# A transformer layer on one core: router chain grouped over several pairs, residual add moved into PSUM, both norms of a pair in one step

## The reference, cut to what matters

```
x = layernorm(x + self_attention(x, causal))           # ln1
x = layernorm(x + cross_attention(x, ctx of 77 rows))  # ln2
p = softmax(x @ router_w + router_b)                   # [2048, 8]
topw, topi = top_k(p, 2);  topw = softmax(topw)
out = sum over the two chosen experts of topw * (gelu(x @ w1[e] + b1[e]) @ w2[e] + b2[e])
x = layernorm(x + out)                                 # ln3
```

## Time and profile before

| | us |
|---|---|
| median of 3 runs | 496.29 (495.0 to 496.47) |
| profiled execution, its own time | 500.52 |
| its span, first to last instruction | 498.5 |
| mean granted TensorE clock | 0.896 |
| iterations with SA, CA and router all at work (starts of SA's last ku): | 124.5, 164.2, 200.7, 236.7, 276.4 |
| POOL's first sending of pairs 0 to 7 | 132.6, 172.2, 208.7, 244.7, 284.3, 318.8, 346.6, 371.2 |

### The profile page before, as it was taken

One profiled execution on the slowest core, in us unless ns is written; L12 is line 12 of the kernel. 1 busy time (PEld: TensorE's weight loads), 2 busy tenths in 40 slices (PEclk: granted clock), 3 DMA queues, 4 the chain that ended last, 5 costly groups with the idle time before them and its releaser, 6 DMA issues.

```text
span 498.5 us, 8885 instructions
## 1 busy us (share of the span) xinstructions
PE 371.4 (75%) x2121; PEld 247.8 (50%) x2121; DVE 315.8 (63%) x1061; ACT 282.5 (57%) x648; POOL 171.4 (34%) x217
## 2 busy tenths in 40 slices
PE   2349678989989989989888998856612999999400
PEld 1313444565455555565464554343212999999300
DVE  9732554778767777878768777546362555555282
ACT  2017268679677769679658769626220555555122
POOL 9403111131431342341422341511311354454343
PEclk9967999999997999999989999975955999999855
DMA  6330202521341332341332331040681122221153
GB/s 196 106 74 0 63 23 49 132 54 33 89 123 31 75 122 44 81 125 35 87 105 48 76 122 39 18 129 19 211 234 48 48 68 66 59 61 51 42 135 84
DMA packets 47818, 39.92 MB, mean 80 GB/s; under 512 B 4762, under 2 KB 44559, under 8 KB 47768
## 3 DMA queue, kind: packets, MB, share of 16 engines
q1 hardware_dynamic: 45496, 35.11, 27.0%
q0 software_dynamic: 2272, 4.24, 2.6%
HBM read 13.66 MB, written 14.79 MB: 57 GB/s over the span
## 4 chain that ended last, share of the span: by engine, by line
PE 31%; DVE 22%; issue 10%; DMA 8%; ACT 8%; SPq 7%; DVEq 7%; POOL 3%; another core or an unknown queue 0%; POOLq 0%; ACTq 0%
PE bank L535 7%; SPq L366 6%; PE bank L479 4%; DMA sa_km<-sa_ku 4%; PE bank L522 4%; DVEq L980 4%; PE bank L480 3%; ACT sa_qm L674 3%; PE bank L503 3%; DVE ca_us L983 2%; PE bank L502 2%; PE bank L546 2%; DVE yb L993 2%; DVE ca_nm L810 2%; ACT ca_qm L674 2%
## 5 line engine op out<-in xcount | busy, mean ns | idle before, releaser
L733 ACT ACTIVATE sa_us<-bank,expert_b 128x128 f32<-128x128 f32 x156 | 44.9, 367 | 47.8 <-PE bank L617 36.1
L1051 POOL TENSOR_SCALAR_AFFINE_SELECT sa_pt<-sa_pt 128x512 f32<-128x512 f32 x64 | 38.9, 635 | 75.8 <-ACT sa_pt L682 75.7
L1083 POOL DMA_INDIRECT results<-sa_us,xs x39 | 41.1, 1054 | 51.8 <-DVE sa_us L995 49.5
L810 DVE TENSOR_REDUCE sa_nm<-bank 128x4 f32<-128x512 f32 x64 | 41.5, 684 | 16.9 <-PE bank L503 16.3
L617 PE MATMUL bank<-xsT,ca_us 128*128 128x128 f32 x312 | 45.7, 291 | 2.6 <-DVE ca_us L983 1.6
L1074 POOL DMA_INDIRECT dispatched<-r_sent,r_row x32 | 31.8, 994 | 44.2 <-DVE r_sent L936 36.9
L674 ACT CAST sa_qm<-bank 8x512 fp32r<-8x512 f32 x64 | 36.9, 576 | 13.7 <-PE bank L510 12.1
L617 PEld LDWEIGHTS bank<-xsT,ca_us 128*128 128x128 f32 x312 | 39.4, 198 | 7.2 <-issue 4.0
L628 PE MATMUL bank<-ca_pt,sa_us 128*128 x312 | 41.5, 276 | 0.2 <-issue 0.2
L674 ACT CAST ca_qm<-bank 8x512 fp32r<-8x512 f32 x64 | 36.8, 575 | 8.2 <-PE bank L510 6.9
L682 ACT ACTIVATE sa_pt<-bank 128x512 f32<-128x512 f32 x64 | 34.8, 597 | 10.1 <-PE bank L522 9.9
(11 more groups left out here) (210 smaller groups left out, 855.9 us busy)
## 6 DMA issues: line engine op xcount, KB each, us to landing
dispatched<-filler SPq DMA_DIRECT2D x17, 520.0 KB, 4.5
sa_km<-sa_ku SPq DMA_DIRECT2D x32, 96.0 KB
sa_qm<-sa_qu SPq DMA_DIRECT2D x32, 96.0 KB
ca_qm<-ca_qu SPq DMA_DIRECT2D x32, 96.0 KB
xs<-dispatched SPq DMA_DIRECT2D x39, 65.0 KB
sa_pt<-in_e_w SPq DMA_DIRECT2D x8, 256.0 KB, 4.8
ca_pt<-in_e_w SPq DMA_DIRECT2D x8, 256.0 KB, 5.5
sa_pt<-results SPq DMA_DIRECT2D x8, 256.0 KB, 4.5
```

What stands on the lines that cost most here:

```text
L733: act.activation(hid[b][:, c, :], bank[2 * b + c // 2][:, P * (c % 2):P * (c % 2) + P], ACT.Gelu, bias=b1[:, bass.ds(expert * FC + c, 1)]) ...
L810: dve.tensor_reduce(k.nm[:, u, g, :], bank[home[k, "scores", u][g % 2]][:, :].rearrange("q (j n) -> q j n", j=J)[:, :, 0:k.keys], AX.X, AL ...
L1051: pool.affine_select(out=blockg, in_=blockg, compare_op=ALU.is_ge, fill=0.0, base=0, pattern=[[0, J], [1, P]], channel_multiplier=-1).then ...
L1083: pool.indirect_dma_start(out=results, out_offset=bass.IndirectOffsetOnAxis(ap=xs[v][:, P:P + 1].bitcast(I32), axis=0), in_=ys[v], in_offs ...
```

## The change

Router: the pairs are put in groups (0, 1), (2, 3, 4), (5, 6) and (7). `route` is still done for each pair, and DVE adds the bias to its logits; everything else of the chain, PE's `place` and POOL's sending included, is done once for a group, when its last pair comes to that step, on tiles of 4, 6, 4 and 2 x 8 values. The chain has 27 instructions beside the one for each pair. The running count goes: PE makes it from products of ones with each earlier group's totals (float32) and with the earlier tiles of the group (bf16). `fill` moves from iteration p + 1 to iteration p + 2 and waits for the sending of the group before its own.

Norm: `residual` is multiplied by the identity into PSUM and wo's product is added on top; for CA the bias bo is added in the same way. Statistics are read from PSUM. Both tiles of a pair are one step: SA's where tile 1 was, CA's at the start of iteration p + 2, where tile 1 was. `x1` goes straight into `residual`, and POOL keeps only one `rs` for both tiles.

```diff
+def routed_together(pairs):
+    groups, left = [], list(range(pairs))
+    for size in (2, 3, 2):
+        if len(left) > size:
+            groups.append(tuple(left[:size]))
+            left = left[size:]
+    return groups + [(p,) for p in left]
...
-        ROUTER_OPS = 32
-        SELECTED = 19
+        SHIFTED, SELECTED, RANKED, ROUTER_OPS = 2, 18, 22, 27
...
-            (CA, "norm", 1, -2), (SA, "weights", 0, 0), (SA, "scores", 3, 0), (SA, "weights", 1, 0),
+            (CA, "norm", 0, -2), (SA, "weights", 0, 0), (SA, "scores", 3, 0), (SA, "weights", 1, 0),
...
-            (SA, "norm", 0, 0), (SA, "values", 0, 1), (CA, "mix", 0, -1), (SA, "turn_heads", 1, 0),
-            (CA, "weights", 1, -1), (SA, "norm", 1, 0), (CA, "weights", 2, -1), (RT, "number", 0, -2),
+            (SA, "values", 0, 1), (CA, "mix", 0, -1), (SA, "turn_heads", 1, 0),
+            (CA, "weights", 1, -1), (SA, "norm", 0, 0), (CA, "weights", 2, -1), (RT, "number", 0, -2),
...
-            (CA, "turn", 0, 0), (RT, "fill", 0, -1), (CA, "mix", 3, -1), (SA, "shift", 0, 1), (CA, "norm", 0, -1),
+            (CA, "turn", 0, 0), (RT, "fill", 0, -2), (CA, "mix", 3, -1), (SA, "shift", 0, 1), 
...
             def fill(k, p, u):
-                if after_pair(p):
-                    sp.wait_ge(r.s_disp, p * 64)
+                first = group_of[p][1][0]
+                if first:
+                    sp.wait_ge(r.s_disp, first * 64)
...
             def norm(k, p, u):                                  # PE
-                pe.wait_ge(k.s_ot, p * 2 + u + 1)
                 take(home[k, "norm", u][0])
-                pe.matmul(bank[home[k, "norm", u][0]][:, 0:D], k.oT[:, u, :], k.wo[:, :], start=True, stop=True).then_inc(k.s_w_ps, 1)
-                give(home[k, "norm", u][0], k.s_y, p * 2 + u + 1)
+                both = bank[home[k, "norm", u][0]][:, 0:2 * D].rearrange("q (v d) -> q v d", v=2)
+                pe.matmul(both, ident, residual[:, 2 * p:2 * p + 2, :], start=True, stop=False)
+                if not k.causal:
+                    pe.matmul(both, ident, k.bo.rearrange("q (o d) -> q o d", o=1).to_broadcast([P, 2, D]), start=False, stop=False)
+                for v in range(2):
+                    pe.wait_ge(k.s_ot, p * 2 + v + 1)
+                    ins = pe.matmul(both[:, v], k.oT[:, v, :], k.wo[:, :], start=False, stop=(v == 1))
+                ins.then_inc(k.s_w_ps, 1)
+                give(home[k, "norm", u][0], k.s_xn, p * 2 + 2)
...
             def place(k, p, u):                                 # PE, once for a group of `tiles` tiles
-                pe.matmul(dst, triangle_bf[:, :], r.sel[:, :, :].rearrange("q v e -> q (v e)"), start=True, stop=False)
-                ins = pe.matmul(dst, ones_bf[:, :], r.acc[:, :, :].rearrange("q v e -> q (v e)"), start=False, stop=True)
+                for c in range(TOPK):
+                    ins = pe.matmul(dst, triangle_bf[:, :], r.chosen[:, c, 0:tiles, :], start=(c == 0), stop=False)
+                for m in range(n):
+                    pe.matmul(dst, ones[:, :], r.total[:, m:m + 1, :].to_broadcast([P, tiles, EXPERTS]), start=False, stop=False)
+                for v in range(tiles - 1):
+                    for c in range(TOPK):
+                        last = v == tiles - 2 and c == TOPK - 1
+                        ins = pe.matmul(dst[:, v + 1:tiles, :], ones_bf[:, :], r.chosen[:, c, v:v + 1, :].to_broadcast([P, tiles - 1 - v, EXPERTS]), start=False, stop=last)
...
             def norm(k, p, u):                                  # DVE
+                dve.wait_ge(k.s_w_ps, p + 1)
+                for v in range(2):
+                    dve.bn_stats(k.bs[:, v, 0:6], y[:, v, :]).then_inc(k.s_bs, 1)
+                if after_pair(p):
+                    dve.wait_ge(k.s_rs, p)
+                for v in range(2):
+                    dve.wait_ge(k.s_bs, p * 2 + v + 1)
+                    dve.bn_aggr(k.ba[:, v, :], k.bs[:, v, :]).then_inc(k.s_ba, 1)
+                for v in range(2):
+                    dve.wait_ge(k.s_ba, p * 2 + v + 1)
+                    dve.scalar_tensor_tensor(out=k.xn[:, v, :], in0=y[:, v, :], scalar=k.ba[:, v, 0:1], in1=k.g, op0=ALU.subtract, op1=ALU.mult).then_inc(k.s_xn, 1)
+                dve.wait_ge(k.s_rs, p + 1)
+                for v in range(2):
+                    dve.wait_ge(k.s_xn, p * 2 + v + 1)
+                    dve.scalar_tensor_tensor(out=residual[:, 2 * p + v, :], in0=k.xn[:, v, :], scalar=k.rs[:, v:v + 1], in1=k.b, op0=ALU.mult, op1=ALU.add).then_inc(k.s_x1, 1)
...
             def norm(k, p, u):                                  # POOL
+                pool.wait_ge(k.s_ba, p * 2 + 2)
+                if after_pair(p):
+                    pool.wait_ge(k.s_x1, p * 2)
+                pool.tensor_tensor(k.rs[:, :], k.ba[:, :, 1], half[:, :].to_broadcast([P, 2]), ALU.pow).then_inc(k.s_rs, 1)
             def number(k, p, u):                                # POOL
+                n, group = group_of[p]
+                if p != group[-1]:
+                    return
                 pool.wait_ge(s_filled, p * 32 + 32)
-                pool.wait_ge(r.s_rt, p * ROUTER_OPS + ROUTER_OPS)
+                pool.wait_ge(r.s_rt, (n + 1) * ROUTER_OPS)
                 pool.wait_ge(r.s_xe1, p + 1)
-                pool.wait_ge(CA.s_xr, p * 2 + 2)
-                for v in range(2):
+                for v in range(2 * len(group)):
                     for c in range(TOPK):
                         pool.indirect_dma_start(out=dispatched, ...
```

More of the change, by code:

```diff
@@ L117, in build @@
         r.xT = sb("r_xT", [D, 2 * P])
[L118 to L127, removed]
+        r.lg, r.ls, r.exl, r.p, r.eq, r.key, r.pm, r.eq2, r.key2, r.base = (
+            sb(f"r_by_expert{n}", [P, TILES, EXPERTS]) for n in range(10))
+        r.nmx, r.sm, r.rsm, r.p1, r.km, r.p2, r.km2, r.d, r.ed, r.den = (
+            sb(f"r_by_token{n}", [P, TILES]) for n in range(10))
+        r.chosen = sb("r_chosen", [P, TOPK, TILES, EXPERTS], BF16)
+        r.at = sb("r_at", [P, TOPK, TILES, EXPERTS])
+        r.pos = sb("r_pos", [P, TOPK, TILES])
+        r.total = sb("r_total", [P, len(ROUTED), EXPERTS])
+        ones = sb("ones", [P, P])
+        r.sent = sb("r_sent", [P, TILES, TOPK, ROW])
+        r.row = sb("r_row", [P, TILES, TOPK], I32)
         r.s_xt_ps = sem("r_xt_ps")
@@ L857, in norm @@
[L857 to L865, removed]
+                y = bank[home[k, "norm", u][0]][:, 0:2 * D].rearrange("q (v d) -> q v d", v=2)
@@ L872, in routed, with wide, each @@
                 ins.then_inc(r.s_rt, 1)
[L873 to L879, removed]
+                dve.wait_ge(r.s_rt, group_of[p][0] * ROUTER_OPS + done[0])
+            def wide(t, tiles):
+                return t[:, 0:tiles].rearrange("q (v o) -> q v o", o=1).to_broadcast([P, tiles, EXPERTS])
+            def each(t, tiles):
+                return t.rearrange("q (o e) -> q o e", o=1).to_broadcast([P, tiles, EXPERTS])
             def gate(k, p, u):
+                n, group = group_of[p]
+                t, at = 2 * len(group), 2 * (p - group[0])
                 if not after_pair(p):
@@ new lines, in second @@
+            def second(k, p, u):
+                n, group = group_of[p]
+                if p != group[-1]:
+                    return
+                t = 2 * len(group)
+                routed(p, dve.scalar_tensor_tensor(out=r.pm[:, 0:t, :], in0=r.chosen[:, 0, 0:t, :], scalar=-2.0, in1=r.p[:, 0:t, :], op0=ALU.mult, op1=ALU.add))
+                largest(p, t, r.pm, r.p2, r.eq2, r.key2, r.km2, 1)
+                routed(p, dve.tensor_tensor(r.d[:, 0:t], r.p2[:, 0:t], r.p1[:, 0:t], ALU.subtract))
+                routed(p, dve.tensor_reduce(r.total[:, n, :], r.chosen[:, :, 0:t, :].rearrange("q c v e -> q e c v"), AX.XY, ALU.add))
@@ new lines, in place @@
+                if p != group[-1]:
+                    return
+                t = 2 * len(group)
+                if group[0]:
+                    dve.wait_ge(r.s_disp, group[0] * 64)
+                dve.wait_ge(r.s_exp, n * 2 + 2)
+                routed(p, dve.tensor_scalar(r.den[:, 0:t], r.ed[:, 0:t], 1.0, None, ALU.add))
+                gates = [r.sent[:, 0:t, c, ROW - 1] for c in range(TOPK)]
+                routed(p, dve.reciprocal(gates[0], r.den[:, 0:t]))
+                routed(p, dve.tensor_tensor(gates[1], r.ed[:, 0:t], gates[0], ALU.mult))
@@ new lines, in place @@
+                routed(p, dve.tensor_copy(r.sent[:, 0:t, :, P].bitcast(I32), rows_sb[:, 2 * group[0]:2 * group[0] + t, :]))
+                assert done[0] == RANKED, done[0]
+            def number(k, p, u):
+                n, group = group_of[p]
+                if p != group[-1]:
+                    return
+                t = 2 * len(group)
+                dve.wait_ge(r.s_rank_ps, n + 1)
+                routed(p, dve.tensor_tensor(r.base[:, 0:t, :], bank[home[k, "place", u][0]][:, 0:t * EXPERTS].rearrange("q (v e) -> q v e", v=t), each(region, t), ALU.add))
```

(4 more changed lines are left out.)

155 lines of the change are left out of this document (67 added, 88 removed).

## The result

The changed kernel takes 522.4 us (median of 4 runs, 520.96 to 526.08) where the kernel before took 496.4 beside it (495.0 to 498.17): ratio 1.0512, interval 1.0472 to 1.0552. That is slower by 25.4 us. The prediction was 513.0 with a range of 499 to 521: the sign was right, the size was not, and the time lies 1.4 us outside the range. The profiled execution of after took 520.96 (span 519.2); the one of before took 500.5, 4 us over its median, so the spans of the two traces are only 20.7 us apart. Sizes are therefore taken from the timed ratios (a ratio less 1, times 496.4), mechanisms from the traces. Each ratio is to runs of the kernel before timed beside it and leaves out runs in which the chip was in a slower state, so that it need not match the medians to 3 us.

A forecast was written before the change was run, and what follows sets the result against it. The prediction took in-order PE to pace the iterations. Its terms, 12.9 + 4.1 + 2.8 + 0.7 - 2.0 - 2.2 + 0.4 = +16.7 us, on 496.3 gave 513, range 499 to 521.

The forecast's parts named there:

- stalls and clock: Group-ending iterations 3 and 6: late fills and long sendings delay rs, PE waits 12.9 us; lowered clock afterwards costs 4.1.
- remaining terms: PE's products +2.8, place +0.7, DVE's relief -2.0, between iterations 7 and 8 -2.2, the end +0.4 us.
- The merged norm: Pair's norm on DVE: 2.6 us where tile 1 alone took 1.9; 0.3 left over, inside the products' 0.46.
- PE's products: Added float32 products: SA's hidden, CA's 0.85 us less 0.4 for ca_y, net 0.46 in six iterations, +2.8 us.
- The gain that was set against them: Dense part: PE's wait for ca_y on bank 5, mostly 0.4 us each time, was set against CA's 0.85.
- DVE's reading from PSUM: Norm's statistics and xn read from PSUM: put at 0; by the Trainium skill's figures 0.26 us more for a pair.
- DVE's relief: 39 us less DVE time, nearly all beside PE's work; only PE's wait for ca_mm counted, about -2.0 us.
- DVE paced after all: Rival, chance 0.11: hidden waits for DVE in PE's busy time make its relief count almost whole; about 488 us.
- Between iterations 7 and 8: DVE's wait for rs of norm 0 behind POOL's sending of pair 5 goes: about -2.2 us.
- The end: Iteration 9: restore 3, bank 5's products, merged norm, shorter chain and place sum to +0.4 us.
- More of all: Rival, chance 0.06: PE's 10.2 us in full, fills at 5.1, clock 7.8; 528 at most, 522 likelier.

The follow-up runs named there:

- e7: The changed kernel with fills after a group's first pair one iteration earlier and POOL's masks made to wait for both x1: 500.5 us, ratio 1.007.
- e11: The whole change with groups of 2, 2, 2, 1, 1, four sendings an iteration, fills as in the kernel before, masks behind x1: 498.5 us, ratio 1.0025.
- e1: The changed kernel with the fills of all but a group's first pair one iteration earlier: 505.5 us, ratio 1.0198.
- e5: The changed kernel with POOL waiting for both x1 after CA's rs, before SA's masks: 516.8 us, ratio 1.0423.
- e3: The kernel before with the new norm alone, router and fill as before: 503.9 us, ratio 1.0169.
- e8: The kernel before with the new norm alone and POOL's masks made to wait for both x1: 498.3 us, ratio 1.002.
- e4: The changed kernel with early fills as in e1 and groups of 2, 2, 2, 1, 1, its own order of masks: 502.4 us, ratio 1.0104.
- e6: The changed kernel with early fills as in e1, groups of 2, 2, 2, 1, 1 and masks behind x1: 513.5 us, ratio 1.03.
- e10: As e8, but PE's product that adds bo left out, so the second norm lacks bo: 495.4 us, ratio 0.9977.
- e9: The kernel before with the router's part alone: groups of 2, 2, 2, 1, 1, four sendings in a row, old norm and fill places: 499.5 us, ratio 1.0002.

## Why the prediction was wrong

By the ratios the loss divides so (the first two lines are differences between kernels that differ in that edit alone; between e7 and e11 the groups and the places and waits of the fills differ too):

```
late fills, stalls and the clock behind them   after - e1    15.6 us
x1 beside the masks                            e1 - e7        6.4 us
rows of sendings, groups, fills' places        e7 - e11       2.2 us
all the rest                                   e11 - before   1.2 us
```

By the intervals of the ratios the lines are uncertain by some 3.4, 3.2, 2.3 and 1.6 us, so that the first two are shown and the last two are not told from nothing. After to e5 and e3 to e8, other ways to the second line, give 4.4 and 7.4, each within some 4; e4 to e6 is the same edit and gives 9.7 the other way, with the late signals that remain open.

Against the forecast: its 17.0 for stalls and clock stand against 17.8 of the first and third lines, its 0 against 6.4, and its remaining terms, -0.3 in sum, against 1.2. That is the 8.7 us between 16.7 and 25.4.

- **Stalls and clock: right in sum, with some luck.** 12.9 + 4.1 = 17.0 forecast, 15.6 + 2.2 = 17.8 measured. The rows of eight and twelve sendings took what was forecast to 0.1 us; the start of the first was right because early fills and a slow landing cancelled. PE got to its transposes at 184.0, not 185.2, as the iteration before was shorter. PE's two waits were 6.95 and 9.46 us, together 16.4 for 12.9, and 3.8 of that are x1 beside the masks (1.92 each). The clock cost more than its 4.1: behind the first stall PE was busy 6.54 us at 0.56, 6.54 x 0.44 = 2.9 us lost, and behind the second 8.25 us at 0.65, another 2.9.
- **The merged norm: the step that failed.** The forecast put x1 beside SA's masks at nothing. It had "two x1 make ... 0.65", from an x1 of 0.35 in the earlier trace rows, and a norm that finished 0.3 us late, inside the 0.46 of its products. It named SA's masks as queued behind rs, and asked only when they would start, not what would run beside them. The old POOL step, a copy of x1, had kept them apart; with the copy gone the masks start in the same instant as x1, and the two x1 take 1.34 to 2.53 us, not 0.65. Cost 6.4 us (4.4 and 7.4 by the other pairs), forecast 0; of the 8.7 us between 25.4 and 16.7 it is the largest part by far. Without it the norm alone costs 1.0 us (e8), where the forecast's terms for it were 2.8 for the products, less 2.2 between iterations 7 and 8, and a part of the 0.4 at the end: the same within the intervals.
- **PE's products.** 2.1 us for one of the two in CA's norm (e10), against 1.4 as half of 2.8: not told apart. The gain that was set against them turned into another wait. PE no longer waits for ca_y on bank 5 (2.3 us before), but for ca_lq 4.3 us in five iterations where it had been 0.8. ca_lq follows ScalarE's ca_hq, which the trace names as what DVE waited for; that this chain bounds the stretch is read from the trace, and no run tests it. DVE's reading from PSUM, put at 0, cost nothing: the statistics take 0.29 us from PSUM as from SBUF, xn 0.34 against 0.38.
- **DVE's relief: too large.** The 2.0 us for ca_mm did not come: 1.9 of the 2.4 are still there, and e9, which has the chain's relief without the norm, shows no gain. DVE was never the bound, as the first paragraph of the forecast said; the rival "DVE paced after all" is excluded by the iteration of 37.07 us with DVE busy for 22.15.
- **Between iterations 7 and 8: right.** From SP's first copy of ca_km for pair 6 to that for pair 7 before took 35.4 us (294.33 to 329.75), e8 32.8: 2.6 for the forecast's 2.2. e3, e10 and e11 have 33.3, 32.4 and 32.6.
- **The end: not settled.** From that copy of pair 7 to the first row load of the slots it was 49.0 us in the trace of before and 52.0 in that of after, +3.0 for the forecast's +0.4. But the same stretch took 48.3 in e1, 49.9 in e5 and 52.0 in e7, which have the same norm, groups and products there, so a single trace doesn't give it to 1 us. On the chain of after stand the four norm products of pair 7 (two lines of 256 columns and wo's) at the lower clock, 2.5 us, and the totals' products of place:

```profile
377.52 0.79 PE bank L573 x2
378.31 0.85 PE bank L575 x2
379.17 0.87 PE bank L578 x4
...
389.02 1.29 PE bank L610 x6
```

- **The chances.** "More of all" was named at 522, for the right time and mostly the wrong reason. Its fills at 5.1 us came near (the second fills took 5.9 and 4.5), and its 7.8 for the clock was 5.8; but its largest term, PE's 10.2 us in full, was not on the path: in e8, which has all those products, the whole norm costs 1.0 us, with an interval that ends at 2.8.

## What to carry to other kernels

When a small instruction goes from an engine's stream, look at what it kept apart. The next in that stream now starts earlier, beside other work, and a DVE instruction with two SBUF inputs next to a GpSimd instruction that reads SBUF is a pair to price before the change is made. A DMA that is asked for by one engine and waited for by another must be moved with both streams in view: here one move by an iteration cost 15.6 us. Work taken from an engine that paces nothing is worth nothing (33 us of DVE time bought no measurable time), so price the relief by the waits of the engine that paces, and ask which wait is next behind each.

## What the runs showed of the hardware

- A DVE instruction of 0.35 us with two SBUF inputs took 0.71, 1.30 or 1.89 beside four masks of 0.62 to 0.68 us in a row on POOL, and ended each time 0.14 to 0.15 us behind the end of a mask. Of two such instructions both were slowed. Which mask lets them in was not tested. In e5, e6, e7, e8, e10 and e11, where the masks wait, every x1 of CA took 0.35, as in the kernel before and in e9.
- POOL sends at an even 1.265 us whether four, eight or twelve stand in a row.
- PE's results can reach DVE and ScalarE 2 to 3.7 us late beside a row of POOL's sendings, in e6 three times, in e8 and e9 once each; in the second stall of after it was 7.1. The trace of before has one such case as well: DVE waited 2.16 us for a signal at 250.60, and the wait of PE at 250.95 in the earlier trace rows, from which the forecast took the price of the low clock, came from it. The cause was not found.
